# Depthwise 3x3 taps of an attention stage as 96x32 diagonal products on row-shifted copies of v, in place of 128x128 products split in two parts

## The reference

```python
proj = xw @ W_qkv + b_qkv                       # q, k, v of every pixel
q_win = q.mean((2, 3)); k_win = k.mean((2, 3))  # one vector for each of the 49 windows
lepe = conv_general_dilated(v_img, lepe_w, window_strides=(1, 1), padding='SAME',
                            feature_group_count=C) + lepe_b      # 3x3, each channel for itself
topk_logit, r_idx = top_k(einsum('npc,nqc->npq', q_win * SCALE, k_win), 4)
# keys and values of the 4 chosen windows: 256 for each window of 64 queries
attn = softmax(einsum('bmqc,bmkc->bmqk', q_h * SCALE, k_sel))
o = einsum('bmqk,bmkc->bmqc', attn, v_sel)
out = (o + lepe) @ W_o + b_o                    # and x + out is the layer's result
```

## Time and profile before

| | us |
|---|---|
| median of 3 runs | 4019.54 (4017.68 to 4019.99) |
| the profiled execution's own time | 4019.97 |
| its span | 4018.2 |
| PE busy | 3715.9 (92%) |
| DVE busy | 2301.8 (57%) |
| ACT busy | 2135.5 (53%) |
| POOL busy | 1671.3 (42%) |
| products of the taps (line 1685), three forms, 504 each | 198.0 + 194.9 + 190.6 |

### The profile page before, as it was taken

One profiled execution on the slowest core, in us unless ns is written; L12 is line 12 of the kernel. 1 busy time (PEld: TensorE's weight loads), 2 busy tenths in 40 slices (PEclk: granted clock), 3 DMA queues, 4 the chain that ended last, 5 costly groups with the idle time before them and its releaser, 6 DMA issues. The chain is left out here.

```text
span 4018.2 us, 108193 instructions
## 1 busy us (share of the span) xinstructions
PE 3715.9 (92%) x31044; PEld 3178.0 (79%) x31044; DVE 2301.8 (57%) x5980; ACT 2135.5 (53%) x5953; POOL 1671.3 (42%) x2962
## 2 busy tenths in 40 slices
PE   7989898989899998969999999999999799978888
PEld 4656566666666665669999999999999688878887
DVE  6868686877778786843333333333333322277777
ACT  5868686877778787844443333333333322045544
POOL 3746373746556464710013333333344311055554
PEclk9999999999999999989999999999999899989999
DMA  4111111111111111111100000000022000000000
GB/s 165 40 55 39 55 40 55 40 54 40 50 44 37 57 40 56 40 64 52 47 37 0 0 0 0 0 0 0 0 63 61 22 0 0 12 17 17 33 33 33
DMA packets 170031, 140.29 MB, mean 35 GB/s; under 512 B 31776, under 2 KB 158368, under 8 KB 166688
## 3 DMA queue, kind: packets, MB, share of 16 engines
q1 hardware_dynamic: 138400, 123.78, 9.4%
q10 hardware_dynamic: 31360, 12.87, 1.2%
HBM read 83.32 MB, written 53.22 MB: 34 GB/s over the span
## 5 line engine op out<-in xcount | busy, mean ns | idle before, releaser
L193 PE MATMUL bank<-h,w_hh 128*128 128x128 f32 x8032 | 933.8, 275 | 0.0
L193 PEld LDWEIGHTS bank<-h,w_hh 128*128 128x128 f32 x8032 | 917.1, 192 | 0.0
L1448 ACT ACTIVATE Pr<-bank,nmx 128x256 f32<-128x256 f32 x1568 | 722.6, 473 | 276.6 <-DVE nmx L1551 270.8
L238 ACT ACTIVATE h<-bank,bg 128x128 f32<-128x128 f32 x1008 | 370.7, 368 | 818.0 <-PE bank L193 817.9
L1385 POOL TENSOR_TENSOR Pr<-Pr,rden 128x512 f32<-128x512 f32 (+1 forms) x784 | 659.6, 855 | 165.9 <-DVE rden L1611 135.8
L1551 DVE TENSOR_REDUCE nmx<-bank 128x1 f32<-128x256 f32 x1568 | 555.1, 417 | 155.6 <-PE bank L1711 154.4
L1375 POOL COPY kg<-kT 128x64 f32 x1568 | 300.2, 238 | 597.2 <-DMA row<-ix 295.2
L284 DVE SCALAR_TENSOR_TENSOR inp<-bank,b_in,tz 128x256 f32<-128x256 f32 x196 | 85.8, 480 | 697.4 <-ACT tz L221 697.4
L1457 ACT ACTIVATE PT<-bank 128x512 f32<-128x512 f32 x784 | 428.8, 610 | 21.4 <-PE bank L1724 21.3
L1724 PE MATMUL bank<-ident,Pr 128*128 128x128 f32 x3136 | 437.5, 283 | 0.0
L1724 PEld LDWEIGHTS bank<-ident,Pr 128*128 128x128 f32 x3136 | 342.7, 143 | 81.1 <-issue 71.7
(11 more groups left out here) (248 smaller groups left out, 7098.0 us busy)
## 6 DMA issues: line engine op xcount, KB each, us to landing
vg<-v_windows SPq DMA_DIRECT2D x1176, 32.0 KB, 2.0
first_gates<-gate_sums SPq DMA_DIRECT2D x28, 512.0 KB, 2.6
gate_sums<-first_gates SPq DMA_DIRECT2D x28, 512.0 KB, 3.6
X<-in_x SPq DMA_DIRECT2D x8, 1568.0 KB, 17.6
vg<-v_windows ACTq DMA_DIRECT2D x392, 32.0 KB, 2.3
x_backup<-X SPq DMA_DIRECT2D x8, 1568.0 KB, 5.9
out<-X SPq DMA_DIRECT2D x7, 1568.0 KB, 5.1
v_windows<-vst SPq DMA_DIRECT2D x56, 192.0 KB, 2.1
```

Of the source, the lines that this page charges most:

```text
L193: ins = pe.matmul(bank[m][:, tt * COLS:(tt + 1) * COLS], w_hh[:, k, m * 128:(m + 1) * 128], prev[:, k, :], start=False, stop=(k == NH - 1) ...
L238: act.activation(h[:, 2 * q + tt, m, :], bank[m][:, tt * COLS:(tt + 1) * COLS], ACT.Tanh, bias=bg[:, 0, m:m + 1]).then_inc(s_h, 1)
L1448: act.activation(Pr[:, par, j, :], bank[j][:, 0:KEYS], ACT.Exp, bias=nmx[:, par, j:j + 1], accum_out=den[:, par, j:j + 1])\
```

## The change

v is written once, unrounded, into one padded picture `vpad`. Transfers on SP's queue copy three row-shifted pictures of a block below each other (`stack`): partition 32 dy + c of strip i holds the rows of channel 32 i + c, shifted by dy. With that one product of a 96x32 matrix (three diagonals, one for each dy) by 448 columns does three taps of 32 channels. Four of them, one for each group of 32 channels, write the four column strips of the array and the four partition quarters of the bank; three such steps (dx = 0, 1, 2) do a block. They are full 32-bit products, and W_o is no longer folded in. The finished block of `lepe` is copied to SBUF (`lp`), added in `attended` where only a multiplication was, and so goes through W_o with the attended values in `out`.

```diff
-            w_tap = [sb(f"w_tap_{k}", [C, 9, C], F32R) for k in ("hi", "lo")]
+            w_tap = sb("w_tap", [STACK, 3 * STRIPS, STRIP])
...
-            vpad = [sb(f"vpad_{k}", [C, H + 2, W + 2], F32R) for k in ("hi", "lo")]
+            vpad = sb("vpad", [C, H + 2, W + 2])
+            vrow = sb("v_rows", [STACK, 2, STRIPS, ROWS, W + 2])
+            lp = sb("lepe", [C, 2, BLK])
...
-            OUT_LAG, ADD_LAG = 2, 3
+            OUT_LAG, ADD_LAG = 3, 4
-            MEAN_AT, VAR_AT = 32, 39
+            MEAN_AT, VAR_AT = 33, 40
+            LEPE_AT = {NWIN * (b - 2) + 6 + dx: (b, dx) for b in range(2, NBLK) for dx in range(3)}
+            COPY_AT = {NWIN * (b - 2) + 9: b for b in range(2, NBLK)}
+            STACK_AT = {3: 2, 8: 3, 12: 4, 18: 5, 25: 6}
...
+                    def stack(n, b, dy):
+                        for i in range(STRIPS):
+                            sp.dma_start(vrow[STRIP * dy:STRIP * dy + STRIP, b % 2, i],
+                                         vpad[STRIP * i:STRIP * i + STRIP, b * ROWS + dy:b * ROWS + dy + ROWS, :])\
+                                .then_inc(s_rep[b % 2], 16)
...
+                            if 1 <= b <= 2:
+                                sp.wait_ge(s_v, n * NBLK + b + 1)
+                                sp.wait_ge(s_lp, n * NBLK + 1)
+                                for dy in range(3):
+                                    stack(n, b - 1, dy)
...
-                        with sp.Fori(0, P2 // 3) as k:
-                            for i in range(3):
-                                gather(k * 3 + i, i)
-                        gather(P2 - 1, (P2 - 1) % 3)
+                        for w in range(P2):
+                            for dy in range(3):
+                                if w - dy in STACK_AT:
+                                    b = STACK_AT[w - dy]
+                                    if dy == 0:
+                                        sp.wait_ge(s_lp, n * NBLK + b)
+                                        sp.wait_ge(s_v, n * NBLK + min(b + 2, NBLK))
+                                    stack(n, b, dy)
+                            gather(w, w % 3)
...
+                        for b in range(2):
+                            act.wait_ge(s_lp, n * NBLK + b + 2)
+                            act.activation(by_row(lp[:, b, :]), bank[7 - b][:, 0:BLK], ACT.Copy).then_inc(s_le, 1)
...
-                    for k in range(9):
-                        dve.tensor_scalar(w_tap[0][:, k, :], w_o[:], lw[:, k:k + 1], None, ALU.mult).then_inc(s_cst, 1)
-                        dve.scalar_tensor_tensor(w_tap[1][:, k, :], w_o[:], lw[:, k:k + 1],
-                                                 w_tap[0][:, k, :].bitcast(F32), ALU.mult, ALU.subtract)\
+                    dve.tensor_tensor(w_tap[:], eye[:].unsqueeze(1).to_broadcast([STACK, 3 * STRIPS, STRIP]),
+                                      lw[:].unsqueeze(2).to_broadcast([STACK, 3 * STRIPS, STRIP]), ALU.mult).then_inc(s_cst, 1)
...
-                            dve.scalar_tensor_tensor(vp[1], vps, vec[:, 2:3], vp[0].bitcast(F32), ALU.add, ALU.subtract)\
...
+                        def copy_lepe(b):
+                            dve.wait_ge(s_lp, n * NBLK + b + 2)
+                            dve.wait_ge(s_o, n * P2 + (b - 1) * NWIN + 1)
+                            dve.tensor_copy(by_row(lp[:, b % 2, :]), bank[7][:, 0:BLK]).then_inc(s_le, 1)
...
-                            dve.tensor_scalar(oh[:], bank[6][:, 0:W2], eo[:, 0:1], None, ALU.mult).then_inc(s_om, 1)
+                            dve.scalar_tensor_tensor(oh[:], bank[6][:, 0:W2], eo[:, 0:1], lp[:, w // NWIN % 2, at],
+                                                     ALU.mult, ALU.add).then_inc(s_om, 1)
...
-                            for i in range(i0, i1):
-                                k, part = divmod(i, 3)
-                                dy, dx = divmod(k, 3)
-                                ins = pe.matmul(bank[7][:, 0:BLK], w_tap[part // 2][:, k, :], vpad[part % 2][at],
-                                                start=(i == 0), stop=(last and i == 26))
+                            for i in range(STRIPS):
+                                ins = pe.matmul(to[STRIP * i:STRIP * i + STRIP, 0:BLK], w_tap[:, dx * STRIPS + i, :],
+                                                vrow[:, b % 2, i, :, dx:dx + W], start=(dx == 0), stop=(dx == 2))
...
-                        lepe(NBLK - 1, 0, 6, False)
+                        for dx in range(3):
+                            lepe(0, dx, bank[7])
                         pe.matmul(bank[1][0:P2, 0:P2], qs[:], ks[:], start=True, stop=True).then_inc(s_lg, 1)
-                        lepe(NBLK - 1, 6, 27, True).then_inc(s_lp, 1)
+                        for dx in range(3):
+                            lepe(1, dx, bank[6])
```

More of the change, by code:

```diff
@@ L49 @@
 QSCALE = float(C) ** -0.5
+STRIP = 32
+STRIPS = C // STRIP
+STACK = 3 * STRIP
 RIN, RH = 256, 512
@@ L1157, in program @@
             s_q, s_k, s_v, s_V = sem("q_ready"), sem("k_ready"), sem("v_ready"), sem("vtok_ready")
-            s_vh = sem("v_hi_ready")
+            s_rep = [sem(f"v_rows_stacked{i}") for i in range(2)]
             s_vst = [sem("v_stored_even"), sem("v_stored_odd")]
@@ L1207, in program @@
             oh = sb("oh", [C, W2])
-            NW = 9
+            NW = 10
             STORED = 32
-            OUT_LAG, ADD_LAG = 2, 3
+            OUT_LAG, ADD_LAG = 3, 4
             STATS_AT = {13: 0, 15: 1, 20: 2, 22: 3, 27: 4, 29: 5, 30: 6}
-            MEAN_AT, VAR_AT = 32, 39
[L1215 to L1226, removed]
+            MEAN_AT, VAR_AT = 33, 40
+            LEPE_AT = {NWIN * (b - 2) + 6 + dx: (b, dx) for b in range(2, NBLK) for dx in range(3)}
+            COPY_AT = {NWIN * (b - 2) + 9: b for b in range(2, NBLK)}
+            STACK_AT = {3: 2, 8: 3, 12: 4, 18: 5, 25: 6}
             def routes(e, w):
@@ L1278, in input_scale, with by_row @@
                 dve.tensor_copy(Bb[:, bass.ds(m, 1)], it).then_inc(s_id, 1)
+            def by_row(t):
+                return t.rearrange("p (w r c) -> p r w c", r=ROWS, c=WIN)
             def following(n):
@@ L1351, in _ @@
                 def _(pool):
-                    for k in range(2):
-                        zero_border(pool, vpad[k][:].unsqueeze(1), s_padz)
-                    for sm in (s_xb, s_V, s_tk, s_kg, s_S, s_O, s_T, s_ev, s_nP, s_ex, s_o, s_Tc, s_mx):
+                    zero_border(pool, vpad[:].unsqueeze(1), s_padz)
+                    for sm in (s_lp, s_xb, s_V, s_tk, s_kg, s_S, s_O, s_T, s_ev, s_nP, s_ex, s_o, s_Tc, s_mx):
                         pool.sem_inc(sm, 1)
@@ L1731, in attend @@
                             pe.wait_ge(s_o, n * P2 + w + 1)
+                            if isinstance(w, int) and w == 0:
+                                pe.wait_ge(s_le, n * NBLK + 2)
                             for j in range(PAIRS):
@@ L1748, in fill @@
                             if w in LEPE_AT:
-                                b, i0, i1 = LEPE_AT[w]
-                                if i0 == 0 and b == 0:
-                                    pe.wait_ge(s_la, n + 1)
-                                elif i0 == 0:
-                                    pe.wait_ge(s_ev, n * NBLK + b + 1)
-                                lepe(b, i0, i1, False)
+                                b, dx = LEPE_AT[w]
+                                if b == 2 and dx == 0:
+                                    pe.wait_ge(s_le, n * NBLK + 2)
+                                elif dx == 0:
+                                    pe.wait_ge(s_ev, n * NBLK + b - 1)
+                                lepe(b, dx, bank[7])
                             b, lag = divmod(w - NWIN, NWIN)
@@ L1814 @@
         "b_q": i["L0_conv_b_qkv"][0:128].reshape(128, 1),
-        "lepe_w": i["L0_conv_lepe_w"].reshape(128, 9),
+        "lepe_w": i["L0_conv_lepe_w"].reshape(4, 32, 3, 3).transpose(2, 1, 3, 0).reshape(96, 12),
         "lepe_b": i["L0_conv_lepe_b"].reshape(128, 1),
```

76 lines of the change are left out of this document (39 added, 37 removed).

## The result

| | before | after |
|---|---|---|
| median in us (runs side by side) | 4019.76 (4017.68 to 4020.17) | 4199.02 (4197.02 to 4201.28) |
| ratio | | 1.0448 [1.0431, 1.0464] |
| span of the profiled execution | 4018.2 | 4195.9 |
| mean granted clock | 0.975 | 0.951 |

Square brackets behind a ratio hold its 95% interval.

What follows compares the result with a forecast made beforehand. PE sets windows with seven taps, the DVE, ACT and POOL chain the others; SP's queue is next fullest. Per image 12 - 4 - 2.3 - 1.0 - 1.5 = 3.2, 8 times 25.6, with the start 30 faster: 3990 us, range 3945 to 4045.

Steps and rivals of the forecast that it cites:

- windows, free of SP: Windows 0 to 47: fewer tap products on PE gain 12 us per image (8 to 13), SP's queue not counted.
- copies in the windows: Windows: 60 transfers per image ahead of gathers on SP's queue stall all engines 4 us per image.
- copies in the projection: Projection: two bursts of twelve copies delay stores, so PE's last projection starts 2.3 us late (0.9 to 5.4).
- logits and clock, without copies: Between the windows: steps put logits 1.0 us later per image, and a lower PE clock costs 1.5 (0 to 4).
- start, once: Kernel start: eighteen tap weights on DVE become one instruction of some 0.5 us, gaining 4.5 us once.
- A copy's price on the queue: SP's queue: each transfer takes 0.45 us, gap included, with bounds 0.39 and 0.58.
- rival 1: SP's queue becomes the bound and eats the gain: 4037 us at 0.52 per copy, 4063 at 0.56; chance 0.24.
- rival 2: SP hides the copies at 0.39 each, no fall of the clock: 77 us faster, 3943; chance 0.17.
- The clock in the windows: Windows: PE's granted clock of 1.00 stays, as short gaps between windows shouldn't change it.
- windows 34 to 47 take more than 45: Sign of being wrong, in windows no copies touch; they were forecast at 43.6 us against 48.2.
- the step of four strips: PE: strips run side by side, 0.85 to 1.0 us per step, taken as 0.95.
- SP's own wait gone: SP's queue: its own wait is near nothing from window 3 to 20.

Runs made afterwards that it cites:

- e1: Changed kernel without all 672 row copies of v and PE's wait on them, taps reading a constant: 3974.85 us, 0.9889 of the kernel before.
- e2: Changed kernel with only the 24 copies per image in the projection, those in the windows left out: 4048.24 us, 1.0071 of the kernel before.
- e3: Changed kernel with only the 60 copies per image in the windows, those in the projection left out: 4119.96 us, 1.0251 of the kernel before.
- e7_shapes: Kernel before plus four transfers each of eight shapes on an empty queue: held 0.59 to 0.60 us with both ends on chip, 0.42 to 0.44 with one in HBM.
- e13: e5_via_hbm with each row fetched in four transfers of 32x464 instead of one: 4124.56 us, 1.0265 of the kernel before.
- e11: Changed kernel with copies of two of the three rows, 448 instead of 672: 4055.08 us, 1.009 of the kernel before.
- e8: e5_via_hbm with tap step, output product or input statistics ahead of attend on PE: 3967.73 us, 0.9878 of the kernel before.
- e12: Kernel before with taps, output product and input statistics moved ahead of attend on PE: 4044.52 us, 1.0064 of the kernel before.
- e5_via_hbm: Changed kernel with v stored to HBM and each row of four strips fetched in one transfer, 28 per image: 3986.11 us, 0.9918 of the kernel before.

## Why the prediction was wrong

Per image, in us; the measured column comes from before, e1, e2, e3 and after:

| step | forecast | measured |
|---|---|---|
| windows, free of SP | +12 (8 to 13) | +6.5 (166.3 - 159.8) |
| copies in the windows | -4 | -19.0 (178.8 - 159.8; e3 alone: 18) |
| copies in the projection | -2.3 | -10.0 (57.96 - 47.95; e2 alone: 9.7) |
| logits and clock, without copies | -2.5 | -0.7 (47.95 - 47.25) |
| start, once | +4.5 | -4.1 |

1. **A copy's price on the queue** is the step that failed first. I bounded it at 0.39 to 0.58 "by the nearest rows", and it is 0.63 (0.633 before rounding; after, e7_shapes). With it the prediction's own formulas give 4 + 60 x 0.183 = 15 and 2.3 + 24 x 0.183 = 6.7, or 8 x (15 + 6.7 + 2.5 - 12) - 4.5 = 93 us slower. So the mechanism and the place were those of rival 1, with the sign of the result, and the price I chose hid them. I gave it 0.24 and stopped its working at 0.56.
2. **The typical price in place of the mean.** e13 shows the windows' loss at 0.46: 10.1, where the formula has 4.8; at 0.63 it is 19 against 15. The slope is right (e11). What is missing are the slow issues. From gather(2) to gather(28) a copy takes 0.69 of the queue on average with its gap in the changed kernel, and 0.55 in e13, because some take 1 to 2 us. With these means the formula gives 4 + 60 x 0.24 = 18.4 and 4 + 60 x 0.10 = 10, against 19.0 and 10.1. Two of the bursts of four in image 1, one as usual and one with a slow issue:

```profile
335.68 2.49 SPq L1307 DMA_DIRECT2D v_rows<-vpad  x4
...
405.95 3.45 SPq L1307 DMA_DIRECT2D v_rows<-vpad  x4
```

   What makes an issue slow is open. The loop's jump, which rival 2 named, does not: 53 of 1176 gathers took over 0.8 in e1, where the loop over the windows is unrolled, and 48 before.
3. **The free gain.** I took a window as the larger of PE's work (3.05) and the chain (3.05 or 3.24). With two nearly equal parts, and PE's idle time at a place where the extra isn't, it is more than either: 3.84 in window 45. The prediction's own check, "windows 34 to 47 take more than 45", came out: 46.0. e8 gave back 3.0 of the missing 5.5; the rest is open.
4. **The projection** has two stalls, of 5.38 and 6.65 on ACT, because both bursts hold a store; I followed only one to its end.
5. **The start.** The projection starts 4.2 earlier (19.32 against 23.5), as forecast. But ACT then waits for the stores of `v_windows` to land. The wait in 24 to 62 us, first of before, then of after:

```profile
ACT vst L1417 <- DMA v_windows<-vst: 4.0, 1, 4.0
```
```profile
ACT vst L1438 <- DMA v_windows<-vst: 13.7, 4, 7.1
```

In e1, without a copy, that wait is 7.5, and PE idles 4.49 and then runs at half speed; the first maximum comes at 61.27. What makes the stores late there, most likely the loads of seven images, I didn't test.

6. **The clock in the windows.** "Short gaps between windows shouldn't change that" failed (0.91 to 0.97 instead of 0.99 to 1.00), at a cost of 1.6 us per image at most in windows 3 to 28.
7. **Slips in the working.** A burst of four at 0.45 is 1.80 and not 1.85, which leaves the stall at 3.6; at 0.39 the same working gives no stall, and not 1; and 3.47 less 0.80 leaves SP 2.7 of work per window and not 2.6. None changes the sign of the forecast.
8. **Right** were the step of four strips (0.89), the logits (2.40), SP's own wait gone, and the places of PE's waits for `vg`. The Trainium skill (DMA: Bandwidth & Descriptors, Issuing engines are not separate DMA queues) calls the time to start a transfer "usually small relative to the DMA itself". The trace disagrees here: 0.63 of the queue per 2.0 of landing, and at 84 transfers more per image it became the bound. The Trainium skill's rule that a change of tiling drains TensorE (TensorEngine Tiling, Key Properties) agrees with e12: 0.18 for one more change per window.

## What to carry to other kernels

Count a queue like an engine: so many transfers by the mean distance of their starts, slow ones included, against the time it waits now. A price that no row shows needs a wider bound than the nearest rows, above all if the ends of the transfer (on chip or HBM) are others than theirs. And when an engine has time over, look where in the window it idles: an extra pays nothing only if it stands there. If four transfers can be one, do that first; it turned 1.045 into 0.992 here, though it took seven stores per image to get there (e5_via_hbm).

## What the runs showed of the hardware

- From start to start on SP's queue, a transfer from on-chip memory to on-chip memory takes 0.63 to 0.65 us, one of 32x464 with an end in HBM 0.46 (e7_shapes). For the first kind neither partitions (32 or 128) nor columns (116 or 464) change it by more than 0.02, and landing is 1.8 to 2.4. Other transfers with an end in HBM hold the queue 0.39 (L1308), 0.47 (gathers) and 0.50 (L1310) in the kernel before.
- Now and then an issue is held much longer: 38 of 672 copies and 45 of 1176 gathers over 0.8 us in the changed kernel, up to 2.1 and 1.7. They lift a copy from 0.63 to 0.69 of queue on average in the windows.
- Four strips of 96x32 with 448 full-precision columns take 0.89 together at a granted clock of 1.00, nearly as little as one product of that length on the whole array (0.85).
- PE's clock after a short idle time is not decided by its length alone. The twelve products ahead of the logits took 4.15 us after 1.57 idle (e8_extras_first, granted clock 0.58 in 262.9 to 267, a mix near the lower level of 1.2 GHz), 4.53 after 6.65 idle (e13_via_hbm_by_strips, 0.52), but 2.46 after 1.49 idle in image 2 of e5_via_hbm (1.00, the level of 2.4 GHz). In e8 alone the steps ran slow behind 1.25 to 1.57 idle in four images, and fast behind 1.03 to 1.98 in the other four. What else decides it is open.
